# Part of the count scatters of a graph kernel moved between the gathers of its first layer

## The chip, the cores and the metric

The kernel runs on one core of one Trainium2 chip. The metric is the device time in microseconds (us), median of several runs. The five engines are TensorE (PE, with its weight loads as PEld), VectorE (DVE), ScalarE (ACT), GpSimd (POOL) and SyncE (SP). Each works through its own list of instructions, and they wait for each other through semaphores.

## The reference, cut to what matters

```python
N_NODES, D, L = 6250, 256, 5           # E = 106250 edges, sorted by dst
norm = dinv[row] * dinv[col]           # dinv = deg ** -0.5
for l in range(L):
    edge_fea = concat([edge_attr[:, 3:] @ ew1[l], edge_attr[:, 0:3] @ ew2[l]])
    msg = norm[:, None] * (h[row] + edge_fea)
    agg = segment_sum(msg, col)
    h = relu(concat([h, agg], 1) @ mlp_w[l] + mlp_b[l])
    h = batchnorm(h) * bn_g[l] + bn_b[l]      # and relu, but for the last layer
x = x + h
x = x + shared_ffn(layernorm(x)) + routed_ffn(layernorm(x))   # 8 experts, top 2
```

## The kernel before, in words

The 6250 nodes make 49 tiles of 128. The sum over the edges of a destination tile is made in one of two ways. For two tiles of every three ("a triple": 16 triples and one tile more), POOL gathers the source rows edge by edge with indirect DMAs, and PE adds them up by a product with a one-hot matrix. A group is four such gathers (K = 4), a quad four groups, so 16 gathers; the ring in SBUF holds four groups (R = 4). For every third tile (the dense tiles, 16 of them, NTR) the kernel first makes a matrix of counts in DRAM, `dense`: how many edges go from each of all nodes to each of the tile's nodes. In the layers PE multiplies these counts with all node rows, which are in SBUF, with no gather.

The counts are made by `scatter_round`: one indirect DMA on POOL adds a one to 128 cells of one dense tile. Each tile gets 20 of them (WIN), one a round, so a round was 16 scatters and there were 320. The semaphores `scattered[q]` count the scatters of four tiles (q = 0 to 3), and a round waits until those of the round before to the same four tiles have landed.

The kernel's beginning is three blocks, with a barrier of all engines between them. The constant `ROUNDS` sets which rounds POOL does in each.

- Block 1 (ends at L383): loads, the plan's bounds, layer norm statistics, degrees. POOL: rounds 0 to 7.
- Block 2 (ends at L666): the first node rows are written to DRAM (`rows0`), the edges are turned, DVE works out the plan. POOL: rounds 8 to 12.
- Block 3 holds all five layers. Ahead of layer 0 PE and DVE make the edge sums of the dense tiles from one-hot products (L1452 to L1483), while POOL does rounds 13 to 19. ACT then waits at L1202 for all four `scattered` and for `edge_summed`, starts the first load of counts (L1205) and enters layer 0.

In a layer ACT makes the indices of each group (`indices`, L1089) once the ring has room, which PE reports with `group_done`; POOL waits for them and issues the four gathers (L1060); DVE makes the one-hot matrices (L1243), PE multiplies (L1516, L1517, L1520). In `triple` on ACT the indices of the groups of a triple stand ahead of `relu_h` (L1104), which waits until PE has mixed the triple before; after it come `load_early` (L1127) and the first indices of the next triple. On PE these mixes stand inside the dense products (L1565, L1567) that follow the triple's shared group. `placed` is a loop whose first instruction is put at a chosen slot of an instruction fetch block.

Of the kernel before, what the change touches and what calls it, by code (L numbers as in the profile page):

```python
# [26 lines left out]
I32 = mybir.dt.int32  # L27
# [7 lines left out]
GG = 4  # L35
# [5 lines left out]
WIN = 20  # L41
# [3 lines left out]
def build(nc, x, src, dst, attr, mlp_w, mlp_b, ew1, ew2, bn_g, bn_b,  # L45
# [9 lines left out]
    NT = -(-N // P)  # L55
# [15 lines left out]
    NTR = NT // 3  # L71
# [4 lines left out]
    WIN_MAX = (E - (P - 1) * WIN - LOOK) // P  # L76
    ROUNDS = (8, 13, WIN)
    assert NT % 3 == 1 and NTR % 4 == 0 and WIN_MAX > 0
# [10 lines left out]
    with ExitStack() as ctx:  # L89
# [3 lines left out]
        def sem(name):  # L93
# [26 lines left out]
        sets = sb("sets", [P, 3 * SET + 1024])  # L120
        scatter_at = sets[:, 3 * SET:3 * SET + NTR * WIN].bitcast(I32).rearrange("p (i j) -> p i j", j=WIN)
        same, clash = (sets[:, 3 * SET + n * NTR * WIN:3 * SET + (n + 1) * NTR * WIN].rearrange("p (i j) -> p i j", j=WIN)
                       for n in (1, 2))
        high_parts = resid[:, :, :].rearrange("p t d -> p (t d)").bitcast(BF16).rearrange("p (t d) -> p t d", d=2 * D)
# [242 lines left out]

        def scatter_round(pool, j):

            for i in range(NTR):  # L370
                if i % 4 == 0:
                    if j == 0:
                        pool.wait_ge(dense_zero[i // 4], 16 * 4)
                    else:
                        pool.wait_ge(scattered[i // 4], 16 * 4 * j)
                pool.indirect_dma_start(dense, bass.IndirectOffsetOnAxis(ap=scatter_at[:, i, j:j + 1], axis=0), one[:], None,  # L376
                                        element_offset=i * ROOM, compute_op=ALU.add).then_inc(scattered[i // 4], 16)
# [5 lines left out]
        with nc.Block() as block:  # L383
# [18 lines left out]
            def _(pool):  # L402
# [29 lines left out]
                for j in range(ROUNDS[0]):  # L432
                    scatter_round(pool, j)

# [231 lines left out]
        with nc.Block() as block:  # L666
# [142 lines left out]
            @block.gpsimd  # L809
            def _(pool):  # L810
                for j in range(ROUNDS[0], ROUNDS[1]):
                    scatter_round(pool, j)

# [144 lines left out]
        rows_stored = [sem(f"rows_stored{i}") for i in range(4)]  # L958

        def placed(engine, kind, a, b, slot):  # L960

# [25 lines left out]
        with nc.Block() as block:  # L987
# [54 lines left out]
            def _(pool):  # L1042
                for j in range(ROUNDS[1], ROUNDS[2]):
                    scatter_round(pool, j)
                quad = counter(pool, "pool_quad")
                steps_h = pool.value_load(plan_h[:, 8 * NU:8 * NU + 1], min_val=1, max_val=NT * MAXG)

                def layer(l, first, final):
                    if not first:
# [3 lines left out]
                        gated(pool)  # L1053
                    with placed(pool, mybir.EngineType.Pool, 0, steps_h, 0):
                        now = pool.snap(quad, min_val=0, max_val=MAX_ALL)
                        for r in range(R):
                            pool.wait_ge(index_ready, now * R + (r + 1))
                            gated(pool)
                            for j in range(r * K, r * K + K):
                                pool.indirect_dma_start(  # L1060
                                    got0_words[:, j, 0:W0 // 2] if first else got[:, j, :], None, rows0 if first else rows,
                                    bass.IndirectOffsetOnAxis(ap=index[:, j:j + 1], axis=0)).then_inc(gathered[r], 16)
                        pool.reg_add(quad, quad, 1)
                    if final:
                        pool.wait_ge(sum_done, l * NT + 3 * NTR)
# [13 lines left out]
            def _(act):  # L1079
# [18 lines left out]
                def layer(l, first, final):  # L1098
# [30 lines left out]

                    def triple(i, head):  # L1130
                        n = start_h(i, 0)
# [13 lines left out]
                        if not head:  # L1145
                            relu_h(i * 3 - 3, 3)
                        load_early(i)

                    def partly_dense():
                        triple(0, True)  # L1150
                        with placed(act, mybir.EngineType.Activation, 1, NTR, 0) as i:
                            triple(i, False)
                        n = start_h(NTR, 0)
# [41 lines left out]
                for i in range(NTR):  # L1195
                    at = act.value_load(starts_i[0:1, i:i + 1], min_val=0, max_val=WIN_MAX * P)
                    for flat, into in ((dst, edge_dst), (src, edge_src)):
                        act.dma_start(into[:, i, :], flat[ds(at, P * WIN)].rearrange("(p j) -> p j", p=P))\
                            .then_inc(edge_win, 16)
                for q in range(4):  # L1200
                    act.wait_ge(scattered[q], 16 * 4 * WIN)
# [1190 lines left out]
```

## Time and profile before

| | |
|---|---|
| median of 3 runs | 6277.48 us (6275.57 to 6286.02) |
| the profiled execution, its own time | 6269.45 us |
| its span, first to last instruction | 6267.7 us |
| PE busy | 4876.1 us (78%) |
| POOL busy | 3669.1 us (59%) |
| DVE busy | 2365.8 us (38%) |
| ACT busy | 901.6 us (14%) |
| block 1 ends at | 371.6 us |
| block 2 ends at | 531.1 us |
| first gather of layer 0 | 768.47 us |
| last gather of layer 0 | 1565.1 us |

Busy time is the time in which an engine carries out instructions that are not register, branch, semaphore or DMA-issuing ones. POOL's indirect DMAs have a duration in the profile and do count as busy. Times in rows are counted from the first instruction of the span.

### The profile page before, as it was taken

To read this page: it belongs to the slowest core of one execution; us is meant where nothing else is said; L and a number is where in the kernel's file an instruction comes from. 1 tells how busy PE (TensorE), PEld (TensorE's weight loads), DVE (VectorE), ACT (ScalarE), POOL (GpSimd) and SP (SyncE) were. 2 spreads that over 40 slices of the span, in tenths; PEclk is the share of its full clock that TensorE was granted. 3 is DMA by queue.
4 is the path that set the end of the run, shared out by engine and by line. 5 is a ranking of instruction groups with operands and counts; after the bars stand their busy time and mean duration, and the time that the engine had idled before them with its cause. 6 is when DMAs were issued, how large, how long until landed. Compare 5 with 4: busy or idle time off the path is not lost. (4 is left out here: it accounts for less than half of the span.)

```text
span 6267.7 us, 117890 instructions
## 1 busy us (share of the span) xinstructions
PE 4876.1 (78%) x26233; PEld 3082.6 (49%) x26234; DVE 2365.8 (38%) x7290; ACT 901.6 (14%) x2478; POOL 3669.1 (59%) x3615
## 2 busy tenths in 40 slices
PE   1402488888588896898986988869889787999998
PEld 0201344555345443454443544434445466888887
DVE  5843745545433334333343333343333531000012
ACT  1610000000200002000021000020000232222222
POOL 2888876767577775777766777757777232000014
PEclk9995599999699997999987999969999888999999
DMA  6263266666566665666656666656666441111113
GB/s 230 0 74 10 25 180 177 179 178 181 153 184 189 192 186 163 187 186 194 186 158 188 186 191 188 188 162 188 194 184 190 140 164 51 60 50 60 49 54 93
DMA packets 461800, 907.25 MB, mean 145 GB/s; under 512 B 157441, under 2 KB 284190, under 8 KB 449134
## 3 DMA queue, kind: packets, MB, share of 16 engines
q0 software_dynamic: 250192, 627.20, 36.9%
q1 hardware_dynamic: 157630, 147.03, 7.5%
q10 hardware_dynamic: 53856, 131.73, 6.2%
q8 instruction: 36, 0.59, 0.0%
q14 instruction: 86, 0.70, 0.0%
HBM read 779.74 MB, written 125.94 MB: 144 GB/s over the span
## 5 line engine op out<-in xcount | busy, mean ns | idle before, releaser
L1060 POOL DMA_INDIRECT sets<-rows,index x2960 | 2801.8, 947 | 1061.8 <-issue 914.3
L1516 PE MATMUL bank<-sets,row_out 128*128 x3280 | 1290.3, 425 | 558.9 <-SPq L1012 441.9
L1565 PE MATMUL bank<-resid,arena 128*128 128x512 bf16 x3920 | 1309.1, 380 | 0.0
L1567 PE MATMUL bank<-sets,arena 128*128 128x256 bf16 x3920 | 1069.8, 273 | 0.0
L1517 PE MATMUL bank<-sets,row_out 128*128 x3280 | 981.4, 299 | 0.0
L1243 DVE TENSOR_SCALAR row_out<-arena,neg_base 128x128 bf16 x2640 | 725.8, 340 | 607.1 <-issue 408.5
L1516 PEld LDWEIGHTS bank<-sets,row_out 128*128 x3280 | 346.6, 106 | 1013.8 <-issue 778.9
L2045 PE MATMUL bank<-sets,arena 128*128 128x256 f32 x2480 | 646.7, 388 | 18.5 <-ACT arena L2061 14.5
L376 POOL DMA_INDIRECT dense<-one,sets x320 | 541.1, 1691 | 199.4 <-issue 96.7
L1565 PEld LDWEIGHTS bank<-resid,arena 128*128 128x128 bf16 x3920 | 383.7, 98 | 519.8 <-issue 105.3
L1089 ACT ACTIVATE index<-arena x740 | 152.3, 206 | 3234.6 <-PE bank L1517 2059.7
L1224 DVE COPY arena<-bank 128x256 f32<-128x256 f32 x245 | 104.0, 424 | 1152.4 <-PE bank L1580 1151.2
L2045 PEld LDWEIGHTS bank<-sets,arena 128*128 128x128 f32 x2480 | 465.3, 192 | 113.2 <-issue 34.0
L2036 PE MATMUL bank<-mix_w,sets 128*128 x1696 | 431.0, 382 | 5.4 <-issue 4.4
L2061 ACT ACTIVATE arena<-bank,bias 128x256 f32<-128x256 f32 (+1 forms) x624 | 293.9, 472 | 864.4 <-PE bank L2036 863.9
L1567 PEld LDWEIGHTS bank<-sets,arena 128*128 128x128 bf16 x3920 | 384.2, 98 | 41.9
L1517 PEld LDWEIGHTS bank<-sets,row_out 128*128 x3280 | 342.6, 104 | 66.3
L1770 POOL DMA_DIRECT2D sets<-in_L_ffn_W1p_dram x6 | 4.3, 725 | 598.4 <-PE bank L2275 598.4
L2036 PEld LDWEIGHTS bank<-mix_w,sets 128*128 128x128 f32 x1696 | 319.7, 191 | 47.8 <-issue 6.4
L2316 POOL DMA_INDIRECT row_out<-expert_out,send_at x98 | 92.7, 946 | 319.8 <-ACT send_at L2326 210.0
L1592 PE MATMUL bank<-feat_t,mix_w 128*128 (+2 forms) x680 | 244.3, 483 | 8.5 <-DVE edge_sum_t L1225 8.5
L1594 PE MATMUL bank<-arena,mix_w 128*128 128x384 f32 (+1 forms) x680 | 242.4, 481 | 0.0
(334 smaller groups left out, 4497.1 us busy)
## 6 DMA issues: line engine op xcount, KB each, us to landing
arena<-dense ACTq DMA_DIRECT2D x80, 1184.0 KB, 6.1
sets<-rows,index POOLq DMA_INDIRECT x2960
arena<-dense ACTq DMA_DIRECT2D x81, 384.0 KB
rows<-resid SPq DMA_DIRECT2D x56, 512.0 KB, 3.0
expert_out<-arena SPq DMA_DIRECT2D x109, 256.0 KB, 2.2
dense<-feat_t SPq DMA_DIRECT2D x16, 1568.2 KB, 46.1
rows<-sets SPq DMA_DIRECT2D x56, 256.0 KB, 3.4
arena<-expert_in SPq DMA_DIRECT2D x54, 256.0 KB, 2.7
```

What stands on the lines that cost most here:

```text
L376: pool.indirect_dma_start(dense, bass.IndirectOffsetOnAxis(ap=scatter_at[:, i, j:j + 1], axis=0), one[:], None, element_offset=i * ROOM, c ...
L1060: pool.indirect_dma_start(got0_words[:, j, 0:W0 // 2] if first else got[:, j, :], None, rows0 if first else rows, bass.IndirectOffsetOnAxi ...
L1243: ins = dve.tensor_scalar(tile(hot, at + j), iota_bf, dst_col[:, ds(c + j, 1)], base, ALU.subtract, ALU.is_equal)
L1516: pe.matmul(to, ones, rows_here[:, ds(from_here + j * wide, 2 * D)], start=start, stop=False)
L1517: mm = pe.matmul(to[:, D:2 * D], ones, rows_here[:, ds(from_here + (j * wide + 2 * D), D)], start=False, stop=stop)
L1565: pe.matmul(bank[:, 5, 0:2 * D], dense_in_sb[:, u * P:(u + 1) * P], high_parts[:, u, :], start=u == 0, stop=False)
L1567: mm = pe.matmul(bank[:, 5, D:2 * D], dense_in_sb[:, u * P:(u + 1) * P], low_parts[:, u, :], start=False, stop=u == NT - 1)
L1592: pe.matmul(o, mix_w[:, k, c], feat_t[:, k, nodes(t, n)], start=k == 0, stop=False)
L1594: pe.matmul(o, mix_w[:, KD + k, c], summed_t[:, k, 0:n * P], start=False, stop=False)
L2036: mm = pe.matmul(bank[:, c % 4, 0:nt * P], w1[:, k, c * P:(c + 1) * P], rows_in(k), start=k == 0, stop=k == KD - 1)
L2045: mm = pe.matmul(bank[:, 4 + u, 0:D], hidden[:, c, u * P:(u + 1) * P], w2[:, c, :], start=c == 0, stop=c == KF - 1)
L2061: act.activation(hidden[:, c, 0:nt * P], bank[:, c % 4, 0:nt * P], ACT.Gelu, bias=bias(c)).then_inc(self.hidden_ready, 1)
```

## The change

The scatters of the last four dense tiles (12 to 15) are taken out of the rounds of the three blocks, so a round is 12 scatters there. Blocks 1, 2 and 3 do rounds 0 to 7, 8 to 10 and 11 to 19 of these. Behind them POOL does four rounds of the last four tiles (16 scatters), enters layer 0, and does the other 16 rounds (64 scatters) one by one behind each of the first 16 quads of gathers. ACT waits for `scattered[3]` only in triple 11 of layer 0, ahead of the load of tile 12's counts. For this POOL's first 16 quads are written out, and ACT's triples of layer 0 are two loops with one triple written out between them; these two loops are plain ones, where the one of before was `placed`. The place of the scatters' indices in SBUF moves behind the ring. Layers 1 to 4 are as before.

```diff
-    ROUNDS = (8, 13, WIN)
+    ROUNDS = (8, 11, WIN)
+    LATE_FROM = 12
+    LATE_AHEAD = 4
...
-        def scatter_round(pool, j):
+        def scatter_round(pool, j, tiles):
-            for i in range(NTR):
+            for i in tiles:
...
                 for j in range(ROUNDS[1], ROUNDS[2]):
-                    scatter_round(pool, j)
+                    scatter_round(pool, j, range(LATE_FROM))
+                for j in range(LATE_AHEAD):
+                    scatter_round(pool, j, range(LATE_FROM, NTR))
...
+                    if first:
+                        for j in range(LATE_AHEAD, WIN):
+                            gathers()
+                            scatter_round(pool, j, range(LATE_FROM, NTR))
+                        with placed(pool, mybir.EngineType.Pool, 0,
+                                    pool.snap(rest, min_val=LEAST + LATE_AHEAD - WIN, max_val=NT * MAXG), 0):
+                            gathers()
+                    else:
+                        with placed(pool, mybir.EngineType.Pool, 0, steps_h, 0):
+                            gathers()
...
+                        if late:
+                            act.wait_ge(scattered[LATE_FROM // 4], 16 * 4 * WIN)
                         load_early(i)
...
-                        with placed(act, mybir.EngineType.Activation, 1, NTR, 0) as i:
-                            triple(i, False)
+                        if first:
+                            with act.Fori(1, LATE_FROM - 1) as i:
+                                triple(i, False)
+                            triple(LATE_FROM - 1, False, True)
+                            with act.Fori(LATE_FROM, NTR) as i:
+                                triple(i, False)
+                        else:
+                            with placed(act, mybir.EngineType.Activation, 1, NTR, 0) as i:
+                                triple(i, False)
...
-                for q in range(4):
+                for q in range(LATE_FROM // 4):
                     act.wait_ge(scattered[q], 16 * 4 * WIN)
```

On POOL, at the end of the scatters of block 3 and the start of layer 0's gathers, before (`plan_h` is the plan with the number of quads):

```order
186 L376 DMA dense<-one,sets 12847104x1 [waits scattered2]
187 L376 DMA dense<-one,sets 12847104x1 x3
188 L376 DMA dense<-one,sets 12847104x1 [waits scattered3]
189 L376 DMA dense<-one,sets 12847104x1 x3
190 L1046 TENSOR_LOAD plan_h
191 L1046 ISA x2
192 L1054 ISA
193 L1054 UNCONDITIONAL_BRANCH
194 L1055 ISA
195 L1060 DMA sets<-rows,index 128x385 [waits index_ready]
196 L1060 DMA sets<-rows,index 128x385 x3
```

The same place in the change:

```order
148 L378 DMA dense<-one,sets 12847104x1 [waits scattered2]
149 L378 DMA dense<-one,sets 12847104x1 x3
150 L378 DMA dense<-one,sets 12847104x1 [waits dense_zero3]
151 L378 DMA dense<-one,sets 12847104x1 x3
152 L378 DMA dense<-one,sets 12847104x1 [waits scattered3]
153 L378 DMA dense<-one,sets 12847104x1 x3
154 L378 DMA dense<-one,sets 12847104x1 [waits scattered3]
155 L378 DMA dense<-one,sets 12847104x1 x3
156 L378 DMA dense<-one,sets 12847104x1 [waits scattered3]
157 L378 DMA dense<-one,sets 12847104x1 x3
158 L1055 TENSOR_LOAD plan_h
```

Four rounds of four scatters now stand between the last full round and the gathers, three of them with a wait for the four scatters right ahead of them. The end of a quad of gathers in layer 0 of the change, still on POOL:

```order
171 L1071 DMA sets<-rows,index 128x385 [waits index_ready]
172 L1071 DMA sets<-rows,index 128x385 x3
173 L1074 REGISTER_ALU
174 L378 DMA dense<-one,sets 12847104x1 [waits scattered3]
175 L378 DMA dense<-one,sets 12847104x1 x3
176 L1066 ISA
177 L1071 DMA sets<-rows,index 128x385 [waits index_ready]
```

Before, the next quad's gathers followed at once; now four scatters (rows 174 and 175) stand between two quads, 16 times. On ACT, where layer 0 goes from triple 11 to its second loop in the change:

```order
430 L1165 COMPARE_AND_BRANCH
431 L1126 ACTIVATE feat_t<-bank,layer_b 128x384 [waits mixed]
432 L1126 ACTIVATE feat_t<-bank,layer_b 128x384
433 L1149 DMA arena<-dense 128x1536 [waits scattered3,dense_used]
434 L1179 UNCONDITIONAL_BRANCH
435 L1179 ISA
```

The wait for the last four tiles' scatters has moved from the entry of the layers to this load.

## Rows read from the trace of the kernel before

**Rows 1.** The page: busy time by engine over the whole span.

```profile
PE 4876.1 (78%) x26233; PEld 3082.6 (49%) x26234; DVE 2365.8 (38%) x7290; ACT 901.6 (14%) x2478; POOL 3669.1 (59%) x3615
```

**Rows 2.** Line L383, block 1's end: durations ns min/median/max, first and last start.

```profile
L383 DVEq DRAIN  x1: 351/351/351, 288.7 to 288.7; - x1
L383 POOLq DRAIN  x1: 24822/24822/24822, 346.8 to 346.8; - x1
```

**Rows 3.** Line L666, the end of block 2, same columns.

```profile
L666 SPq DRAIN  x1: 7/7/7, 448.1 to 448.1; - x1
L666 DVEq DRAIN  x1: 833/833/833, 451.5 to 451.5; - x1
L666 POOLq DRAIN  x1: 27606/27606/27606, 503.3 to 503.3; - x1
L666 SPq EVENT_SEMAPHORE  x1: 17/17/17, 531.1 to 531.1; - x1
```

**Rows 4.** Scatters (L376) alone by stretch: length, POOL busy (count), clock, DMA share, GB/s.

```profile
114.70:309.90 195.20, 165.88 (x96) 1.00 0.27 0
372.40:444.20 71.80, 60.88 (x36) 1.00 1.06 145
531.70:755.20 223.50, 190.56 (x108) 0.54 0.31 8
```

**Rows 5.** Timeline, 367 to 769 us: start, duration, instruction, idle before and its releaser.

```profile
367.42 1.55 POOL L376 DMA_INDIRECT dense<-one,sets  x1 [0.30 <-issue]
...
752.42 2.58 POOL L376 DMA_INDIRECT dense<-one,sets  x1 [0.30 <-issue]
755.31 1.55 POOL L376 DMA_INDIRECT dense<-one,sets  x1 [0.31 <-issue]
...
764.67 0.36 DVE L1483 TENSOR_TENSOR edge_sum<-bank,dinv 128x192 f32<-128x192 f32 x1 [0.80 <-PE bank L1716]
...
768.47 1.03 POOL L1060 DMA_INDIRECT sets<-rows,index  x1 [6.06 <-ACT index L1089]
```

**Rows 6.** Gathers (L1060) alone, quads 1 to 16 and 17 to 37 of layer 0.

```profile
768.40:1117.10 348.70, 242.35 (x256) 0.90 0.63 178
1117.10:1566.10 449.00, 317.94 (x336) 0.96 0.63 181
```

**Rows 7.** All gathers of layer 0: durations ns min/median/max, first and last start.

```profile
L1060 POOL DMA_INDIRECT sets<-rows,index x592: 942/946/1033, 768.5 to 1565.1; - x198
```

**Rows 8.** Timeline in layer 0, 906 to 915.5 us, around one wait of POOL.

```profile
909.54 0.95 POOL L1060 DMA_INDIRECT sets<-rows,index  x1 [0.30 <-issue]
910.33 1.05 ACT L1104 ACTIVATE feat_t<-bank,layer_b 128x384 f32 x2 [9.30 <-PE bank L1595]
910.79 0.95 POOL L1060 DMA_INDIRECT sets<-rows,index  x1 [0.30 <-issue]
...
911.79 0.35 ACTq L1127 DMA_DIRECT2D arena<-dense  x1
...
914.05 0.21 ACT L1089 ACTIVATE index<-arena  x1 [2.67 <-issue]
...
915.06 0.94 POOL L1060 DMA_INDIRECT sets<-rows,index  x1 [3.32 <-ACT index L1089]
```

**Rows 9.** All engines by stretches: PE, PEld, DVE, ACT, POOL busy, clock, DMA share, GB/s.

```profile
768.00:814.00 46.00, 22.98 (x123) 12.38 (x121) 15.10 (x76) 2.22 (x10) 34.15 (x36) 0.65 0.65 187
814.00:860.00 46.00, 37.17 (x215) 21.46 (x216) 22.16 (x97) 1.64 (x8) 32.47 (x35) 0.93 0.64 175
906.00:952.00 46.00, 39.24 (x246) 23.05 (x244) 23.30 (x100) 2.91 (x11) 32.62 (x35) 0.96 0.64 183
```

**Rows 10.** The same for 7 us at either clock.

```profile
897.00:904.00 7.00, 6.44 (x40) 3.95 (x40) 3.56 (x16) 0.20 (x1) 5.46 (x6) 1.00 0.61 155
786.00:793.00 7.00, 5.66 (x24) 2.68 (x24) 3.73 (x18) 0.41 (x2) 5.17 (x7) 0.50 0.58 158
```

**Rows 11.** DMA queues with any packet from 880 to 1560 us.

```profile
q0 software_dynamic: 32294, 99.52, 52.6%
q10 hardware_dynamic: 22185, 23.52, 10.5%
```

**Rows 12.** DMA issues, whole span, another indirect scatter: count, median us to landing.

```profile
expert_in<-row_out,send_at POOLq DMA_INDIRECT x98, 2.6
```

More of the change, by code:

```diff
@@ L120, in build @@
         sets = sb("sets", [P, 3 * SET + 1024])
-        scatter_at = sets[:, 3 * SET:3 * SET + NTR * WIN].bitcast(I32).rearrange("p (i j) -> p i j", j=WIN)
+        scatter_at = sets[:, 3 * SET + 1024 - NTR * WIN:3 * SET + 1024].bitcast(I32).rearrange("p (i j) -> p i j", j=WIN)
         same, clash = (sets[:, 3 * SET + n * NTR * WIN:3 * SET + (n + 1) * NTR * WIN].rearrange("p (i j) -> p i j", j=WIN)
-                       for n in (1, 2))
+                       for n in (0, 1))
         high_parts = resid[:, :, :].rearrange("p t d -> p (t d)").bitcast(BF16).rearrange("p (t d) -> p t d", d=2 * D)
@@ L811, in _ @@
                 for j in range(ROUNDS[0], ROUNDS[1]):
-                    scatter_round(pool, j)
+                    scatter_round(pool, j, range(LATE_FROM))
             @block.tensor
@@ L958, in build @@
         rows_stored = [sem(f"rows_stored{i}") for i in range(4)]
+        LEAST_TRIPLE = 2 + 1 + 1 + 1 + 1
+        LEAST = -(-NTR * LEAST_TRIPLE // GG)
+        assert WIN - LATE_AHEAD < LEAST and (WIN - LATE_AHEAD) * GG <= LATE_FROM * LEAST_TRIPLE
         def placed(engine, kind, a, b, slot):
@@ L1043, in _ @@
                 for j in range(ROUNDS[1], ROUNDS[2]):
-                    scatter_round(pool, j)
+                    scatter_round(pool, j, range(LATE_FROM))
+                for j in range(LATE_AHEAD):
+                    scatter_round(pool, j, range(LATE_FROM, NTR))
                 quad = counter(pool, "pool_quad")
-                steps_h = pool.value_load(plan_h[:, 8 * NU:8 * NU + 1], min_val=1, max_val=NT * MAXG)
+                rest = counter(pool, "pool_rest")
+                steps_h = pool.value_load(plan_h[:, 8 * NU:8 * NU + 1], min_val=LEAST, max_val=NT * MAXG)
+                pool.reg_add(rest, steps_h, LATE_AHEAD - WIN)
                 def layer(l, first, final):
@@ L1053, in layer, with gathers @@
                         gated(pool)
-                    with placed(pool, mybir.EngineType.Pool, 0, steps_h, 0):
+                    def gathers():
                         now = pool.snap(quad, min_val=0, max_val=MAX_ALL)
@@ L1128, in load_early, with triple @@
                             .then_inc(dense_early, 16)
-                    def triple(i, head):
+                    def triple(i, head, late=False):
                         n = start_h(i, 0)
```

## The prediction

> **What bounds the kernel now.** The page comes first: no engine is busy all the time [rows 1], so shares of the span say nothing about this change, and each stage has to be read for the wait that ends it. The change touches four stages.
>
> Block 1: the two drains at its end show who is late. DVE, the last of the others, is done at 288.7 + 0.4 = 289.1 us; POOL's drain ends at 346.8 + 24.8 = 371.6 us [rows 2]. The last scatter ended at 367.42 + 1.55 = 368.97 us [rows 5], so the block closes 2.65 us behind POOL's last scatter. All others wait about 82 us for scatters.
>
> Block 2: DVE is done at 451.5 + 0.8 = 452.3, SP at 448.1, POOL at 503.3 + 27.6 = 530.9 us, and the block opens at 531.1 [rows 3]. Again some 78 us of waiting for scatters.
>
> Block 3 ahead of layer 0: here the chain of DVE and PE ends at 764.67 + 0.36 = 765.0 us, with the last scatter of 112 about there too, and the first gather starts at 768.47 us, released by ACT's index [rows 5]. In this stage fewer scatters buy nothing: after 108 of them, at 755.2 us [rows 4], DVE still has 10 us to go.
>
> Layer 0: a gather takes 0.946 us [rows 7] and the next starts 0.30 us later [rows 8], 1.25 us in all. 256 gathers are 320.0 us of the 348.7 us that the first 16 quads take, 336 are 420.0 of 449.0 us [rows 6]. So POOL issues almost without a pause, and layer 0 is bound by it; PE is busy for 39.2 of 46 us [rows 9]. What POOL does beside gathers in layer 0 is therefore not free. Its 28.7 and 29.0 us of waiting are the only slack. One such wait is in [rows 8]: ACT sat 9.30 us for PE's mix, then did the relu, the load and, at 914.05, the index; POOL had run dry and stood for 3.32 us. It is a chain that begins with the gathers of the shared group: PE needs its rows, then multiplies and mixes, then ACT goes on, while POOL has only the three groups behind the shared one to issue (15 us).
>
> **The change part by part.**
>
> *Block 1.* 96 scatters instead of 128. The first 96 end at 309.9 us [rows 4]; with the same 2.65 us the block closes at 309.6 + 2.65, about 312.3 us, instead of 371.6: -59.3 us. DVE's 289.1 us lies well ahead of it. A round's wait now looks back over 8 scatters instead of 12, at least 14.8 us; an indirect scatter lands in 2.6 us [rows 12], so no new wait.
>
> *Block 2.* 36 scatters instead of 80. They take 71.8 us [rows 4] plus 2.65 for the drain, 75 us from the block's start, while DVE needs 452.3 - 371.8 = 80.5 us. So DVE closes it, at 452.5 us on the old clock instead of 531.1: -78.6 us. From here on fewer scatters would buy nothing in this block either.
>
> *Block 3, up to the first gather.* The 108 scatters end at 755.2 us, ahead of DVE's chain (765.0), so ACT enters layer 0 as before. But POOL has 16 more to do. At 1.85 us a scatter (1.55 + 0.30, [rows 5]) they are 29.6 us; some stretch to 2.58 us beside DVE's large operations [rows 5], for which I add 1 us. Three of the four rounds wait for the scatters right ahead of them. The nearest rows for that wait: the drain of 2.65 us behind the last scatter, less the 0.30 us of pause that is there anyway, 2.35 us; at least nothing, at most 2.6 us of landing [rows 12] plus 0.5 for the wake-up (from ACT's index, done at 914.26, to the gather at 915.06, less the usual 0.30, [rows 8]). I take 2.35 x 3 = 7 us. The first gather starts at 755.3 + 30.6 + 7 = 792.9 instead of 768.5 us: +24.4 us (17 to 27). The load of the plan is issued while POOL works and costs nothing; it stood there before.
>
> *Layer 0, first 16 quads.* 64 scatters at 1.85 us: +118.4 us. The upper bound is block 3's rate, 223.5 / 108 = 2.07 us [rows 4]: 132 us. I stay at the low end, because the gathers keep to 942 to 1033 ns beside layer 0's DVE work [rows 7], where the scatters beside block 3's do not.
>
> The Trainium skill speaks against that choice: "SBUF — State Buffer", section "SBUF: two separate sides", says that VectorE in a two-port mode and GpSimd hold one pair of ports against each other for a whole instruction. By it the scatters would be slowed in layer 0 too, and the sum would stand at the 132 us end; the gathers' narrow spread speaks for short holds only.
>
> The slack of 28.7 us is given back against this. The chain of [rows 8] runs from the shared group's gathers, with four places between groups until POOL needs the next index; exactly one of any four in a row is the end of a quad, and now holds 7.4 us of scatters. That is more than the 3.32 us wait. I count -28.7 us, and +2 for chains that PE's lower clock after longer idling makes longer. What cover there is, is used up by this: were the waits not hidden, the 28.7 us would come back.
>
> *Layer 0, the other 21 quads.* The wait for `scattered[3]` comes in triple 11, some 25 quads in, with the last scatter in quad 16: no cost. Nothing else changes there, and the 29.0 us of waits stay. Layers 1 to 4 and the rest are the same instructions.
>
> Sum: -59.3 - 78.6 + 24.4 + 118.4 - 28.7 + 2 = -21.8 us. Of 138 us gained at the two barriers, 116 go back in layer 0, because POOL is the bound there. Against the profiled execution's own 6269.45 us that gives 6247.7; this execution lies 8 us below the median of the runs shown (6277.48), which would give 6255.7. I say 6254.
>
> **The rivals.**
>
> *The waits stay.* The ring stall and the scatters may not overlap: if PE itself is behind at these places (39.2 us busy of 46, [rows 9]), POOL stands as long as before. Speaks for it: the stalls come once a triple with PE always busy. Against: PE gets 57.8 us for the work of 46 (below). Time: -21.8 + 26.7 = +5, 6282; no change.
>
> *ACT's loops fetch their code again.* The loop of ACT in layer 0 is no longer placed, and a fetch at each turn would stand between `load_early` and the next index, in the middle of the chain of [rows 8]. Hidden in the first 16 quads, it shows in some 9 turns behind them; by the nearest short DMA, 2.6 us [rows 12], +23 us: 6278, no change. Against it: from 880 to 1560 us only q0 and q10 move packets [rows 11], so no engine fetched instructions in 14 turns of loops, VectorE's among them, whose body is 2.6 times as long as ACT's in the built program and crosses more of its code. The Trainium skill, "Runtime: NRT & Kernel Launch", section "Instruction fetch mechanics", says that a taken branch to code outside the window held forces a fetch; by that rule this rival is what happens, if ACT's body falls badly.
>
> *PE becomes the bound at the lower clock (slower).* In the first 16 quads PE will idle more, and rows show what idling does: 0.65 mean clock with 23 us busy of 46, 0.93 with 37 [rows 9]. 46 us of now hold 16 x 46 / 348.7 = 2.11 quads; with scatters POOL needs 2.11 x (20 + 7.4) = 57.8 us for them. PE's 39.2 us must grow 1.47 times to reach that. At 1.2 GHz a matmul took 5.66 / 24 = 0.236 us against 6.44 / 40 = 0.161 at 2.4 GHz [rows 10], 1.47 times, and at most 2 times. So it decides only if the clock stays at 1.2 GHz nearly throughout. With 1.7 times: (66.6 - 57.8) x 7.6 triples = 67 us, 6254 + 67 = 6321. Against it: the dense products are long busy stretches, after which the clock was at 2.4 GHz each time, and PE's share of 39.2 / 57.8 = 68% lies between the two rows, so about 0.8 of the clock.
>
> *Scatters slower in layer 0.* At 2.07 us and with the longest landing waits: +14 + 2.3, 6270, still a little faster or level.
>
> **How the numbers follow.** Forecast 0.60; waits stay 0.12; fetches 0.08; PE's clock 0.08; slow scatters 0.08; something in blocks 1 and 2 not gained as read 0.04. What this kernel's measurement can tell from no change is about 0.2%, 12.6 us. Faster by more than that: the forecast with nearly all its own range (6240 to 6265) and a part of the slow scatters, 0.66. Within: the waits, most of the fetches, the rest of the scatters, 0.20. Slower: the clock, the far ends of waits and fetches, 0.14. The range: low end, no landing waits (-7), no residual (-2) and some of the later waits gone too (-6), 6239, against the profiled run's lower level a few us less; high end, waits stay plus half of the fetch price, 6290. I give 6237 to 6290.
>
> **What would show it.** Block 1 closing at about 312 us and block 2 about 81 us later with DVE's drain last; the first gather some 261 us behind the opening of block 3 (before: 237); the first 16 quads taking about 440 us with scatters at 1.85 us and almost no wait for ACT's index; the other 21 quads at 449 us; layers 1 to 4 unchanged. Wrong would make it: waits for ACT's index of 3 us a triple in the first 16 quads, instruction packets between 900 and 1500 us, a clock near 0.5 in those quads, or scatters at 2 us.

## The result, and the profile after

The changed kernel takes 6269.33 us (median of 20 runs, 6259.65 to 6286.73), the kernel before beside it 6281.89 us (20 runs, 6267.45 to 6290.67). The medians lie 12.6 us apart; the ratio of all the runs is 0.9984, 95% interval 0.9977 to 0.9992, so some 10 us faster (5 to 14), where 22 were forecast. The profiled execution of the changed kernel took 6260.89 us itself, its span is 6259.0 us. The page says that the mix of work is the same as in [rows 1]:

```profile
PE 4864.0 (78%) x25939; PEld 3081.1 (49%) x26234; DVE 2358.4 (38%) x7290; ACT 901.6 (14%) x2478; POOL 3671.1 (59%) x3615
```

The two barriers, as in [rows 2] and [rows 3] (the lines are L385 and L668 now; durations ns min/median/max, first and last start):

```profile
L385 DVEq DRAIN  x1: 351/351/351, 288.7 to 288.7; - x1
L385 POOLq DRAIN  x1: 24079/24079/24079, 291.4 to 291.4; - x1
```

```profile
L668 POOLq DRAIN  x1: 23937/23937/23937, 374.4 to 374.4; - x1
L668 DVEq DRAIN  x1: 769/769/769, 394.7 to 394.7; - x1
L668 SPq DRAIN  x1: 7/7/7, 402.3 to 402.3; - x1
L668 SPq EVENT_SEMAPHORE  x1: 17/17/17, 402.5 to 402.5; - x1
```

Block 1 closes at 315.5 instead of 371.6 us, POOL last again. Block 2 lasts 86.9 instead of 159.3 us. DVE is done where it was forecast (79.9 us after the opening), POOL's drain ends at 398.3 (10.5 us behind its last scatter, where 2.65 were forecast), and SP comes last, at 402.3. The waits of SP in that stretch (us in total, times, longest) say for what:

```profile
SPq L683 <- DVE sets L719: 27.4, 10, 6.0
SPq L689 <- DMA attr_rows<-arena: 10.6, 1, 10.6
```

The stretches of scatters, and the gathers of layer 0, as in [rows 4] and [rows 6] (length, POOL busy (count), clock, DMA share, GB/s):

```profile
114.70:309.80 195.10, 165.89 (x96) 1.00 0.32 0
315.60:387.90 72.30, 60.83 (x36) 1.00 1.26 123
402.50:667.40 264.90, 215.30 (x124) 0.54 0.37 13
667.50:1109.00 441.50, 100.42 (x64) 0.82 0.62 139
```

```profile
667.50:1109.00 441.50, 243.67 (x256) 0.82 0.62 139
1109.00:1558.00 449.00, 317.01 (x335) 0.95 0.64 180
```

In the first 16 quads POOL is busy for 243.67 + 100.42 = 344.1 of 441.5 us, and 320 pauses of 0.30 us are the other 96: it issues without a stop. Its waits there (total us, times, longest) have no entry longer than the usual pause, so the stalls of [rows 8] are gone:

```profile
POOL sets L1071 <- issue: 74.0, 243, 0.3
POOL dense L378 <- issue: 18.9, 62, 0.3
POOL sets L1071 <- ACT index L1111: 4.0, 13, 0.3
```

The last part to be read is the 16 new scatters ahead of the gathers (timeline, as in [rows 5]):

```profile
631.83 1.55 POOL L378 DMA_INDIRECT dense<-one,sets  x1 [0.30 <-issue]
636.07 1.98 POOL L378 DMA_INDIRECT dense<-one,sets  x1 [2.69 <-DMA dense<-one,sets]
...
645.94 1.55 POOL L378 DMA_INDIRECT dense<-one,sets  x1 [2.33 <-DMA dense<-one,sets]
...
660.16 1.55 POOL L378 DMA_INDIRECT dense<-one,sets  x1 [7.12 <-DMA dense<-one,sets]
...
667.57 1.03 POOL L1071 DMA_INDIRECT sets<-rows,index  x1 [0.30 <-issue]
```

Three waits for the scatters right ahead, as forecast. They are 12.1 us, of which 11.2 lie beyond the usual 0.30 us pause; 7 were forecast. The first gather starts 265.1 us after block 3 opens (before 237.4).

So by the profiled execution: -56.1 (block 1), -72.4 (block 2), +27.7 (to the first gather), +92.8 (first 16 quads), +1.4 (the others; 450.3 us from the start of the first to the end of the last gather, before 448.9). That is -6.6 us at the last gather of layer 0, against -21.8 forecast.

The +1.4 is one pause. In both kernels POOL has a pause of up to 2.07 us once in 520 gathers, for which the profile shows no releaser. Before, its place in layer 0 is in the first 16 quads; in the change it is in quad 37. The timelines, before and after:

```profile
1064.12 0.94 POOL L1060 DMA_INDIRECT sets<-rows,index  x1 [2.07 <-issue]
```

```profile
1541.03 0.94 POOL L1071 DMA_INDIRECT sets<-rows,index  x1 [2.07 <-issue]
```

### The profile page after: what moved, and what is told of

Same layout as the page of the kernel before. It is cut to its first block and busy times, and to the rows that moved or that the text cites. A ratio compares the mean times of both kernels' runs of the same rounds, so it can differ in the third digit from the quotient of the medians.

```text
span 6259.0 us, 117567 instructions
## 1 busy us (share of the span) xinstructions
PE 4864.0 (78%) x25939; PEld 3081.1 (49%) x26234; DVE 2358.4 (38%) x7290; ACT 901.6 (14%) x2478; POOL 3671.1 (59%) x3615
## 5 line engine op out<-in xcount | busy, mean ns | idle before, releaser
L1596 PE MATMUL bank<-resid,arena 128*128 128x512 bf16 x3700 | 1257.1, 382 | 0.0
```

The lines of the kernel that those rows point to most:

```text
L1596: pe.matmul(bank[:, 5, 0:2 * D], dense_in_sb[:, u * P:(u + 1) * P], high_parts[:, u, :], start=u == 0, stop=False)
```

## The experiments

Eighteen runs on five chips: r1 to r4 on chip A, r5 to r8 on B, r9 to r12 on C, r13 to r16 on D, r17 and r18 on E. The kernels on one chip share its runs of before. On chips A and C the gathers of each of layers 1 to 4 take 960 to 1030 us where they take 755 in the profile of before, and layer 0 is longer too, so what happens in layer 0 has other sizes there; chips B, D and E ran like the profile of before. This table has the stages of the traces of the latter, one execution each: block 1's close, block 2's length, the first gather after the opening of block 3, the two groups of quads, the start of layer 0's last gather, the span (all in us), and the ratio of the timed runs to before with its interval. A dash stands where a kernel had a single run; "change" without a label is the result above.

| kernel | block 1 | block 2 | 1st gather | quads 1-16 | 17-37 | last gather | span | ratio |
|---|---|---|---|---|---|---|---|---|
| before | 371.8 | 159.3 | 237.4 | 348.7 | 448.9 | 1565.1 | 6267.7 | |
| before, r14 | 371.4 | 160.0 | 237.8 | 344.9 | 448.9 | 1562.1 | 6271.7 | - |
| plain_loop, r18 | 371.5 | 159.5 | 238.1 | 355.1 | 451.7 | 1575.0 | 6286.0 | 0.9995 (0.9985-1.0006) |
| change | 315.6 | 86.9 | 265.1 | 441.6 | 450.3 | 1558.5 | 6259.0 | 0.9984 (0.9977-0.9992) |
| change, r13 | 315.6 | 80.0 | 263.9 | 442.2 | 463.8 | 1564.6 | 6258.8 | 0.9973 (0.9963-0.9983) |
| waits_moved, r15 | 315.2 | 79.9 | 263.4 | 441.5 | 457.6 | 1556.7 | 6260.8 | 0.9964 (0.9949-0.9978) |
| no_late, r16 | 315.3 | 79.9 | 237.7 | 350.7 | 460.9 | 1443.6 | 6171.5 | - |
| ahead_mixed, r5 | 315.6 | 79.9 | 254.8 | 441.6 | 455.8 | 1546.9 | 6252.4 | 0.9956 (0.9939-0.9972) |
| mixed_12, r6 | 315.7 | 98.9 | 238.8 | 441.9 | 455.2 | 1549.5 | 6245.6 | 0.9968 (0.9955-0.9982) |
| two_a_quad, r7 | 315.8 | 80.0 | 285.5 | 389.9 | 480.7 | 1551.0 | 6258.8 | 0.9949 (0.9932-0.9965) |
| one_a_group, r8 | 315.6 | 79.9 | 255.8 | 445.8 | 454.7 | 1551.0 | 6255.1 | 0.9962 (0.9948-0.9976) |
| mixed_placed, r17 | 315.1 | 79.9 | 254.2 | 441.6 | 450.7 | 1540.5 | 6248.4 | 0.9965 (0.9951-0.9978) |

**Is POOL the bound, and were SP's stores one execution's? (r1 to r4, r9 to r11, r13 to r16.)** Two kernels beside the change, each on chips A, C and D. r1 and r14 are the kernel before again, r2, r9 and r13 the change again.

*no_late* (r3, r11, r16) leaves out the 80 late scatters and ACT's wait for them in triple 11. The counts of tiles 12 to 15 stay zero, so their part of the output is not that of the reference; the rest of layer 0 runs as it does:

```diff
-                for j in range(LATE_AHEAD):
-                    scatter_round(pool, j, range(LATE_FROM, NTR))
...
                             gathers()
-                            scatter_round(pool, j, range(LATE_FROM, NTR))
```

*waits_moved* (r4, r10, r15) takes SP's waits for its stores from the end of block 2 to the engines that need the stores:

```diff
-                sp.wait_ge(row0_stored, 16 * (2 * NR0 + 1))
-                sp.wait_ge(attr_stored, 16)
...
+                    if first:
+                        pool.wait_ge(row0_stored, 16 * (2 * NR0 + 1))
...
+                act.wait_ge(attr_stored, 16)
```

> The kernel before, once more, for the lengths of its stages. In its first profile block 1 closed 2.65 us behind the last scatter, block 2 5.4 us behind it, and SP was done 76 us into block 2. Theory A (POOL's own work from the first scatter to the last gather is the bound, and what its stages lose between them is fixed by the program): block 1 at 371 to 375 us, block 2 159 to 163 us long, SP done 76 to 78 us into it. Rival B (SP's stores of the first rows take a varying time, whatever the kernel): SP done anywhere from 76 to 88 us into block 2, with the block's length still set by POOL.

> The changed kernel once more. Theory A: SP's stores again close block 2, 86 to 88 us after its opening; first gather of layer 0 265 us after the opening of block 3; 6250 to 6270 us, 10 us under before. Rival B: SP is done at 76 to 80 us, DVE closes block 2 at 80.5 us, and the whole is 16 us under before.

> The 80 scatters of the last four dense tiles are left out altogether, so those tiles' counts stay zero. Theory A (each late scatter costs POOL 1.85 us in layer 0, hidden only as far as POOL waited there, 28.7 us): blocks 1 and 2 as in the change (-56 and -73 us against before), the first gather 237 us behind block 3's opening, the first 16 quads at 348 us again: 128 us under before, 6153 us. Rival C (the scatters in layer 0 are nearly free and the gain is lost at the barriers): no more than 40 us under before.

> SP no longer waits at the end of block 2 for its stores of the rows and of the edge attributes; POOL waits for the rows ahead of its first gather and ACT for the attributes ahead of its first load of them. Theory A: block 2 then closes with DVE at 80.5 us or with SP's last issue, up to 6 to 11 us earlier than in the change, and the whole gets faster by as much, since POOL is the bound behind it: 6 us (0.1%) under the change. Rival D (block 3's chain of DVE and PE or something later takes it back): within 2 us of the change.

Chip A, with before at 7696.12 us (7 runs): r1 7703.25; r2 7647.66, ratio 0.9922 (0.9895 to 0.9949); r3 7545.59, 0.9814 (0.9785 to 0.9843); r4 7644.32, 0.9922 (0.9899 to 0.9946). POOL has more slack in layer 0 on this chip. Its waits in the first 16 quads, before (r1) and in the change (r2):

```profile
POOL sets L1060 <- ACT index L1089: 157.7, 36, 8.6
```

```profile
POOL sets L1071 <- ACT index L1111: 91.3, 26, 8.4
```

The 64 scatters hid in waits, the 16 quads grew by 58.9 us only (467.2 to 526.1), and the change gained 60 us and not 10. Without the late scatters (r3) the 16 quads took 468.2 us, as before, so the scatters were the 58 us. Block 2 was 79.9 us in r2 and r4. So SP's late end was not there, and waits_moved had nothing to gain.

> The changed kernel once more, since the first profile of it had a block 2 of 87 us, closed by SP's stores, and four other profiles with the same block had 80 us, closed by DVE. Theory B (slow stores are a rare event of a single execution): block 2 80 us, first gather 264 us behind it, first 16 quads 441 us; 14 to 17 us (0.22 to 0.27%) under before on a chip with layers of 755 us. Rival G (they come in a good part of its executions): block 2 near 87 us or its timed runs spread by 7 us more than before's, and 10 us under before.

> The change with SP's waits for its stores moved out of block 2, on a chip with layers of 755 us. Theory B: SP is not the one that closes block 2, 80 us, and the time is that of the change within 3 us. Rival G: 3 to 7 us under the change.

> The 80 scatters of the last four dense tiles left out, on a chip with layers of 755 us (the first such run had layers of 1020 us and showed 58 us for the 64 scatters in layer 0). Theory A: first 16 quads 347 to 350 us, so the 64 scatters cost 93 us of their 118; the whole 56 + 79 = 135 us under before. Rival C: first 16 quads at 400 us or more, so the stalls do not come back without the scatters.

> The kernel before with ACT's loop over the triples of layer 0 as a plain loop, as in the change. Rival (each turn fetches its code again): instruction packets on q14 all along layer 0 and 2.6 us more for each of 15 turns, layer 0's gathers 839 instead of 798 us. Theory A (the fetch blocks are held whatever their place): 796 to 801 us and no instruction packets between 900 and 1500 us.

Chip C has the long layers too (before 7517.40 us, 11 runs): r9 7453.1, 0.9924 (0.9900 to 0.9948); r10 7454.97, 0.9925 (0.9903 to 0.9947); r11 7375.68 and r12 7509.0, one run each. It repeats chip A and says nothing of a chip like that of the prediction. r12 is plain_loop, shown below; its one run is 8 us under the median of before, and its trace has no instruction packet on q14 between 900 and 1500 us.

> The changed kernel again, hoped for on a chip with layers of 755 us. By the stages of the runs so far (block 1 at 315.5, block 2 80 us, first gather 264 us behind it, first 16 quads 441.5 us, the rest 450 to 455 us) it should be 13 to 17 us under before. Theory B (the 87 us block 2 of the first profile was one execution): that. Rival G (slow stores come often): 8 to 11 us under before.

> The kernel before once more: blocks 371.7 and 159.3 us, first gather 237 us behind, first 16 quads 349 us, the other 21 449 us by the first profile. Theory A: each within 2 us. Rival H (the 21 later quads vary by 5 us, which would be a third of what is looked for): 449 to 455 us.

> SP's waits for its stores out of block 2. Theory B: within 3 us of the change; block 2 80 us. Rival G: 3 to 7 us under it.

> The 80 late scatters left out; on a chip with layers of 755 us: first 16 quads 347 to 350 us (Theory A), so that the scatters there cost 93 of 118 us; rival C: 400 us or more.

Chip D is like that of the prediction (before 6279.18 us, 13 runs): r13 6261.36, r15 6260.1 us; r14 6273.47 and r16 6173.2, one run each. Block 2 in r13 (the drains, as in [rows 3]):

```profile
L668 POOLq DRAIN  x1: 27633/27633/27633, 367.0 to 367.0; - x1
...
L668 SPq DRAIN  x1: 7/7/7, 393.0 to 393.0; - x1
L668 DVEq DRAIN  x1: 767/767/767, 394.7 to 394.7; - x1
```

DVE closes it after 80.0 us, as in nine further traces of kernels with 36 scatters in the block; on chip C it was 82 to 83 us, with POOL last. The 86.9 us of the first profile are one execution's. SP waits 6.7 us for its stores in r13, but is done 2.5 us ahead of DVE; moving the waits away (r15) changed nothing that can be measured.

By r13's and r16's traces the 16 scatters ahead cost 263.9 - 237.7 = 26.2 us, the 64 others 442.2 - 350.7 = 91.5 us of the 118.4 that they occupy. So the scatters that were moved still cost 118 of the 135 us that the barriers gave. These are single executions: without scatters there, the first 16 quads took 344.9, 348.7, 350.7 and 355.1 us in the four traces of the table. The whole time says less (6173.2 us, one run, 88 under the change). From layer 0's last gather to the end no_late takes 6171.5 - 1443.6 = 4727.9 us, 34 more than r13, with other values in its data; why is not known, so its stages are compared and not its total.

The surprise is in the quads behind them. no_late does nothing there that before doesn't, but for the form of the loops, and takes 460.9 us for 448.9. The changed kernels take 450.3, 463.8 and 457.6. That is what r17 and r18 are about.

**Can the places be better? (r5 to r8.)** *ahead_mixed* (r5) puts each ahead round behind one of the last four full rounds, so that no round waits for the four scatters right ahead:

```diff
                     scatter_round(pool, j, range(LATE_FROM))
-                for j in range(LATE_AHEAD):
-                    scatter_round(pool, j, range(LATE_FROM, NTR))
+                    if j >= ROUNDS[2] - LATE_AHEAD:
+                        scatter_round(pool, j - (ROUNDS[2] - LATE_AHEAD), range(LATE_FROM, NTR))
```

The other three are made on it. *mixed_12* (r6) has `ROUNDS = (8, 12, WIN)`, one more full round in block 2. *two_a_quad* (r7) has eight rounds ahead, four scatters behind the first quad and two behind each of the next 22:

```diff
-    LATE_AHEAD = 4
+    LATE_AHEAD = 8
...
+                        for j in range(LATE_AHEAD + 1, WIN):
+                            for a in (LATE_FROM, LATE_FROM + 2):
+                                gathers()
+                                scatter_round(pool, j, range(a, a + 2))
```

*one_a_group* (r8) puts one scatter behind each group of four gathers:

```diff
+                            if late is not None:
+                                scatter_round(pool, late, range(LATE_FROM + r, LATE_FROM + r + 1))
```

> The change, but its four early rounds of the last four tiles stand behind the last four full rounds in turn, so that twelve other scatters lie between two rounds to the same tiles. Theory A (the 12 us that POOL stood for landings between those rounds is lost time, since POOL is the bound): no wait for a landing any more, first gather 251 to 255 us behind block 3's opening instead of 263 to 265; 10 us (0.15%) under the change. Rival D (something else closes this stage at once, as ACT's entry behind the last full round): first gather at 260 us or later.

> The same, and block 2 does four full rounds instead of three (48 scatters). Theory A: POOL's pause at the end of block 2 (15 us in the first profile of the change) shrinks to its drain of 5 to 7 us: block 2 about 103 us long and closed by POOL, block 3 with 12 scatters fewer and its first gather at 238 to 240 us, now closed by the chain of DVE and PE and ACT's index (233 + 4 us). Against the run with mixed rounds alone: 103 - 80 + 239 - 253 = +9 us where SP's stores are quick (block 2 80 us), +2 us where they are slow (87 us). Rival E (POOL's pauses at the barrier are the loss that the change brought): faster by 8 us or more than the mixed rounds alone.

> As the mixed rounds, but with eight rounds ahead, and the other 48 scatters two behind each of 22 quads (four behind the first). Theory A (a bundle of any length over 3.3 us swallows the stall of its quad, so 23 quads hide 41 us where 16 quads hide 29): on a chip with layers of 755 us, about 10 us under the mixed rounds: first gather at 283 us, no waits for ACT's index in 23 quads, 1.25 us a gather. Rival F (what a bundle hides is set by its length): no better than the mixed rounds. On a chip where quads take 29 us anyway: at most 9 us a quad can be hidden, two scatters hide wholly: the whole 10 to 30 us under the mixed rounds.

> As the mixed rounds, but each late round's four scatters stand one behind each group of a quad instead of four at its end. Theory A: the same work and the same slack in any four groups: first 16 quads 441 us as in the change, within 3 us of the mixed rounds on a chip with layers of 755 us. Rival F (it is the closed bundle that hides a stall or that starves PE): a difference of more than 5 us in the first 16 quads.

Chip B, with before at 6273.10 us (10 runs): r5 6249.08, r6 6251.32, r7 6246.96, r8 6248.94. In r5 POOL's waits from the opening of block 3 to the first gather have no entry for its own scatters any more, only the usual pauses and the barrier:

```profile
POOL dense L378 <- issue: 37.5, 123, 0.3
POOL dense L378 <- POOLq L668: 8.4, 1, 8.4
```

The first gather comes 9.1 to 10.3 us earlier than in the change. One more full round in block 2 (r6) makes the block 98.9 us (19 more) and the stage behind it 16 us shorter, 3 us worse on balance. Two scatters behind a quad (r7) hide less. In its first 16 quads POOL waits for ACT's index 7.4 us where the change waits 4.0 (all of it pauses), in the rest 37.7 us:

```profile
POOL sets L1072 <- ACT index L1115: 7.4, 15, 1.3
```

```profile
POOL sets L1072 <- ACT index L1115: 37.7, 17, 6.4
```

So 3.7 us of scatters behind a quad cover a stall all but 1.3 us, but 16 more scatters went ahead of layer 0, where nothing hides them (+30.7 us at the first gather, -26.8 in the quads). One behind each group (r8) costs 4.2 us more in the first 16 quads, between what the two sides had expected. The intervals of the four ratios overlap, so the timed runs don't rank them; the traces put them 7.5 to 11.7 us ahead of the change at the last gather (and r17, whose POOL does the same as in r5, 18).

**Why do quads 17 to 37 take longer? (r17, r18, and r12.)** Two causes were left: the rival "ACT's loops fetch their code again", since ACT's two loops in layer 0 are no longer placed, or a PE that is slower in some triples. *mixed_placed* (r17) is ahead_mixed with both loops placed:

```diff
-                            with act.Fori(1, LATE_FROM - 1) as i:
+                            with placed(act, mybir.EngineType.Activation, 1, LATE_FROM - 1, 0) as i:
...
-                            with act.Fori(LATE_FROM, NTR) as i:
+                            with placed(act, mybir.EngineType.Activation, LATE_FROM, NTR, 0) as i:
```

*plain_loop* (r12, r18) is the kernel before with layer 0's loop on ACT plain:

```diff
-                        with placed(act, mybir.EngineType.Activation, 1, NTR, 0) as i:
-                            triple(i, False)
+                        if first:
+                            with act.Fori(1, NTR) as i:
+                                triple(i, False)
+                        else:
+                            with placed(act, mybir.EngineType.Activation, 1, NTR, 0) as i:
+                                triple(i, False)
```

> The kernel with the ahead rounds mixed in, and ACT's two loops of layer 0 placed as the loops of the other layers are. Theory J (the clock): in quads 17 to 37 the change's traces have stalls of 5 to 6 us where before they are 3 us, and each long one lies in a stretch of 50 us whose granted clock is 0.90 or 0.93 and not 0.97; which turns it hits differs from execution to execution, and code loading has no part. Then the instruction packets between 880 and 1560 us go away and nothing else: long stalls stay, one to six of them, each in a stretch at 0.90 to 0.93, quads 17 to 37 take 450 to 464 us, ratio 0.995 to 0.998. Rival C (ACT's loops fetch their code again): quads 17 to 37 fall to 449 us, every stall but one is 3 us whatever the clock, and the ratio falls by 0.001 against the same kernel with plain loops (0.9956), to 0.9945.

> The kernel before, with ACT's loop of layer 0 plain and nothing else changed. Theory J: ratio 0.999 to 1.001, quads 17 to 37 stay within 447 to 460 us, and long stalls stand where the clock is 0.90. Rival C: 2.6 us a turn in 15 turns, up to 39 us more, ratio 1.003 to 1.006, and POOL's waits for ACT's index grow in every second quad of layer 0.

Chip E, with before at 6278.36 us (15 runs): r17 6252.03 us, r18 6273.0 us (10 runs). A plain loop in the kernel before costs nothing (0.9995, interval up to 1.0006, where the rival said 1.003 to 1.006). Placed loops give the change nothing (0.9965, where it said 0.9945). The packets don't follow the placing either: from 882 to 1550 us the queues of r18, plain, move none of instructions (its two queues come first below), while r17, placed, has 6 of them between 900 and 1500, as the first profile of the change, plain, has:

```profile
q0 software_dynamic: 31553, 97.21, 52.9%
q10 hardware_dynamic: 21461, 23.09, 10.8%
```

```profile
q14 instruction: 6, 0.05, 0.0%
```

The rival falls. What is left can be read from the stalls themselves. In quads 17 to 37 POOL stands still once in two quads, nearly always 3 us, in some triples 5 to 6. Kernel before, the stalls that end at 1352 and at 1402 us, timeline:

```profile
1352.38 0.95 POOL L1060 DMA_INDIRECT sets<-rows,index  x1 [3.33 <-ACT index L1089]
...
1402.42 0.94 POOL L1060 DMA_INDIRECT sets<-rows,index  x1 [5.29 <-ACT index L1089]
```

And the same kernel in 11 us some 25 us ahead of either (busy times: PE, PEld, DVE, ACT, POOL busy, clock, DMA share, GB/s):

```profile
1323.00:1334.00 11.00, 5.34 (x31) 2.95 (x29) 6.36 (x30) 0.62 (x3) 8.48 (x9) 0.84 0.78 253
1376.00:1387.00 11.00, 7.72 (x35) 3.99 (x36) 6.83 (x32) 0.41 (x2) 8.42 (x9) 0.54 0.61 160
```

PE is granted 0.84 in the one and 0.54, nearly all at the lower of its two levels (1.2 GHz), in the other. In r13, which has six long stalls, three stretches at the lower level, and one in which it was short:

```profile
1221.00:1232.00 11.00, 8.36 (x39) 4.44 (x41) 6.84 (x31) 0.20 (x1) 8.26 (x10) 0.53 0.62 161
1272.00:1283.00 11.00, 9.09 (x42) 4.85 (x44) 7.00 (x31) 0.41 (x2) 8.25 (x10) 0.53 0.62 161
1323.00:1334.00 11.00, 8.99 (x42) 4.82 (x43) 6.95 (x31) 0.41 (x2) 8.26 (x10) 0.53 0.60 160
1422.00:1433.00 11.00, 7.91 (x49) 4.76 (x51) 7.03 (x33) 0.62 (x3) 8.26 (x10) 0.84 0.62 161
```

The stalls that follow them add 5.2, 5.4, 5.6 and 3.0 us to the usual pause. The third in the timeline:

```profile
1347.91 0.96 POOL L1071 DMA_INDIRECT sets<-rows,index  x1 [5.92 <-ACT index L1111]
```

Over the traces of the table but r7 there are 99 such stalls, counting those that add over 2 us to the usual pause. In the 32 us ahead of its end a stall of under 4 us had at most 6.8 us at the lower level (69 of 69), one of over 4 us at least 10.2 us of it (27 of 30). Before has one long stall in each of its two traces, plain_loop two, the kernels with fewer barrier scatters 1, 1, 2, 3, 4, 4, 5 and 6. Each is 2 to 3 us longer than a short one. The stalls of r13, with six long ones, come to 12.0 us more than those of before; with the 1.8 us of the pause in quad 37 that is nearly all of its +14.9.

The clock's part is shown by this count, which is a correlation, and not by an edit. What makes a stretch at the lower level 3.4 or 10.2 us long was not found, nor whether the changed kernels have more long ones by their nature. The chips speak against that in part: on the chip of the result the change has one, as before has, and on chip E r17 has one and plain_loop two. The many come from chips D (6, 4 and 5, where r14, before, has one) and B (4, 3 and 2, with no trace of before).

## Why the prediction was off

The sign and the mechanism were right: the barriers gave what was read, and POOL paid most of it again. The size was not: 10 us (5 to 14) for 21.8. Several terms of the sum were too favourable. Too small in every trace of the change were the drain of block 1 (2.65 us, measured 5.8 and more) and the landing waits ahead of layer 0 (7 us, measured 7.8 to 11.2). The term that was put at nothing, the other 21 quads, had no other ground than "nothing else changes there"; it measured +1.4 to +14.9. Step by step:

- **Block 1, -59.3:** -56.1. The step "with the same 2.65 us" failed by 3.2. POOL's drain ended 5.8 us behind its last scatter in the change (5.8 to 6.6 in all traces of changed kernels, 2.6 to 3.0 in the five of kernels with 128 scatters in the block; why is open). The profile of before had nearly this number at its other barrier, which the prediction left out. There the last scatter ends at 523.98 + 1.55 = 525.5 us and the drain at 530.9, 5.4 us behind:

```profile
523.98 1.55 POOL L376 DMA_INDIRECT dense<-one,sets  x1 [0.30 <-issue]
531.82 1.55 POOL L376 DMA_INDIRECT dense<-one,sets  x1 [6.29 <-POOLq L666]
```

- **Block 2, -78.6:** -79.3 in r13, with DVE last as the prediction had it; -72.4 in the first profile, because of SP in that execution. That POOL would be done at 75 us fits neither: its drain ended 6.7 us behind the last scatter in r13 and 10.5 in the first profile, and on chip C it closed the block.
- **To the first gather, +24.4:** +27.7 and +26.5. The three waits for landing were 11.2 us beyond the pauses and not 7 (in r13 9.2, in r15 7.8). The forecast took the barrier's 2.65 us for each, which fits two of the three (2.69, 2.33) but not the third (7.12). r5, without the waits, is 9.1 to 10.3 us earlier. These 24.4 us lie ahead of layer 0, though the prediction counts them in the 116 that go back "in layer 0".
- **First 16 quads, +118.4 - 28.7 + 2 = +91.7:** +92.8 and +93.5, and the scatters ran at 1.85 us. The stalls are swallowed, so "The waits stay" fell, and with it "Scatters slower in layer 0" (100.42 / 64 = 1.57 us a scatter there). The other traces of before put these 16 quads at 344.9 and, with the plain loop, 355.1 us, so a miss of 2 us is within what one execution differs from the next.
- **What lengthens a scatter** was left open by the prediction. In the trace of before 70 of the 320 scatters took over 1.65 us, and 69 of them began while a TENSOR_TENSOR of DVE of 1.17 to 2.81 us was running, and ended 1.42 to 1.44 us behind it. The TENSOR_REDUCE of 1.17 us, with one input, lengthened none of the 16 scatters that began beside it. One such pair:

```profile
738.09 2.81 DVE L1473 TENSOR_TENSOR row_out<-arena,sets 128x2560 bf16<-128x2560 bf16 x1
739.75 2.58 POOL L376 DMA_INDIRECT dense<-one,sets  x1 [0.30 <-issue]
```

In layer 0 DVE's TENSOR_TENSOR take some 0.2 us, and the scatters stay at 1.57. The Trainium skill's "SBUF — State Buffer", section "SBUF: two separate sides", by which a VectorE operation with two SBUF inputs and a GpSimd operation that reads SBUF hold each other up for the whole instruction, agrees with these 69 scatters. In layer 0 it has no price, so its use for the 132 us end was wrong.
- **PE's clock, the slower rival:** granted 0.82 in those quads, between 0.65 and 0.93 of [rows 9] and near the 0.8 worked out, and POOL didn't wait. It fell as the price of +67 us in the first 16 quads. In the quads behind them the lower level goes with the longer stalls, and in r13 these are the largest single miss.
- **Other 21 quads, 0 ("the 29.0 us of waits stay"):** +1.4, +14.9, +8.7 in three traces of the change or its near twin r15; over all changed kernels but r7, 1.4 to 14.9. This step failed. 1.8 us of it is the pause of 2.07 us that came from the first 16 quads to quad 37, the rest longer stalls: they stayed 3 us only where PE's stretches at the lower level stayed short.
- **"ACT's loops fetch their code again":** the symptom named for it, instruction packets between 900 and 1500 us, did come, a handful (6 on q14), but also with placed loops, and the placing had no price: r17 and r18. The Trainium skill, "Runtime: NRT & Kernel Launch", section "Instruction fetch mechanics", has a taken branch out of the window force a fetch; no run here shows such a fetch on a critical path.

By these terms r13 misses by 3.1 - 0.7 + 2.1 + 1.8 + 14.9 = 21.2 us and ends level with before at the last gather of layer 0 (1564.6 for 1565.1). The first profile misses by 3.2 + 6.2 + 3.3 + 1.1 + 1.4 = 15.2. What the timed runs have beyond that can't be placed by traces: from the last gather of layer 0 to the end, the same instructions took 4702.6 and 4709.6 us in the two traces of before and 4700.5, 4694.2 and 4704.1 in the change (twice) and r15, a spread of 15 us, as large as the gain. Whether the 6.5 us between the means are the change's or chance stays open. Over all the changed kernels of the table but no_late this part takes 4694.2 to 4707.8 us, which overlaps before. On chip D the gap is plain: r13's trace is 2.5 us behind that of r14 at the last gather, while the medians there put the change 17.8 us ahead. So where the timed gain of any chip lies is not shown stage by stage.

The forecast's base was off too: the 6254 mixed a profiled execution with a median of three runs that lay 4 us below the one of twenty.

## What to carry to other kernels

Work that is moved off a barrier on the engine that is also the bound behind it gains only what it fills of that engine's pauses: 135 us came off the barriers, and no_late shows some 118 of them paid again. Price a drain and a landing from every place where the profile has one, not from the nearest: 2.65 and 5.4 us stood in the same trace, and 5.8 came. A stage in which POOL has only 3 us of waiting a triple for a chain through PE can grow with PE's clock, so its time is a range (449 to 464 us here), also where its instructions don't change.

## What the runs showed that I had not expected

- Two of the five chips ran the gathers of layers 1 to 4 in 960 to 1030 us a layer and not 755, before and change alike, with POOL waiting for ACT's index 157.7 us in 16 quads instead of 35.8. On them the same change gained 0.75 to 0.8%, since its scatters hid in those waits. Why these chips are slower is not known.
- PE's granted clock in layer 0 drops to the lower level for 3.4, 6.8 or 10.2 us at a time although its work is the same from quad to quad, and where 10.2 us of it stand ahead of a stall, the stall is 2 to 3 us longer. The twenty timed runs of the change point the same way: the two with the lowest mean clock over the whole span (0.886 and 0.887) are the two longest (6286.73 and 6285.56 us), the one with the highest (0.897) takes 6259.69.
- A wait for an indirect scatter that adds to memory took 2.69, 2.33 and 7.12 us within 30 us on one queue, and 2.00, 1.82 and 6.31 us in r13.
